# The causal mask of the first score pass moved from TensorE into VectorE's maximum

## The chip, the cores and the metric

The kernel runs on one core of one Trainium2 chip, in one launch. The metric is the device time of that launch in microseconds; the kernel before took 659.16 us (median of three runs, 657.58 to 659.57).

## The reference, cut to what matters

The program is a small network on x of shape 8 x 256 x 16 x 16: a non-local convolution block, a quantised convolution block, and two transformer layers over 256 tokens of 256 channels in each of 8 batches. Both layers attend causally with 16 heads of 16 channels; the first adds a linear bias (ALiBi) before the mask:

```
scores = einsum('bhqd,bhkd->bhqk', q, k) / sqrt(16)   (+ slope_h * (key - query), first layer)
scores = where(key <= query, scores, -inf)
attn   = softmax(scores, axis=-1)
out    = einsum('bhqk,bhkd->bhqd', attn, v)
```

The first layer is followed by a ternary linear layer, the second by a mixture of eight experts with top-2 routing.

## The kernel before, in words

**Two attention passes.** The softmax needs the largest score of each query. The kernel computes the scores twice. The first pass (pieces "S") has queries on the 128 partitions and keys along the free dimension; VectorE reads the scores from PSUM and reduces them to one negated maximum per query and head. These maxima (tile `nmax`) are split into two bf16 parts (pieces "MS", tile `nparts`), turned by TensorE (pieces "M") and copied by ScalarE into extra rows of the stacked queries `QS`. The second pass (pieces "X") has keys on the partitions, includes the negated maximum as one more product row, and ScalarE takes the exponential out of PSUM.

**Units.** The 16 heads form 4 groups of 4. Each group has three units in the first pass, each filling one PSUM bank of 512 columns: part 0 holds the first 128 queries of four heads (128 keys each, as later ones are masked); parts 1 and 2 hold the second 128 queries of two heads each (256 keys each). The mask is a product: TensorE multiplies an identity by a table (`tri0`, `tri1`) of 0 and -1e30 into the bank, and the score products accumulate on top. In parts 1 and 2 this mask product covers the second 128 keys of both heads (256 columns, line 1230); then come two score products of 256 columns (line 1235). One VectorE instruction (line 1467) takes both heads' maxima out of the bank.

**Bodies and the order of work.** There are 16 bodies: 8 batches of layer one ("stage 0", which also carries its ternary layer as stage 1) and 8 of layer two ("stage 2", with the experts as stage 3). The order of each engine's work is written out at build time by `in_order`: every piece has a step, bodies follow each other every 12 steps, and so the pieces of two or three bodies interleave. Each engine runs its own list in order and waits on semaphores. Six PSUM banks are handed round the pieces in TensorE's order: a piece may write its bank only when the one six before has been drained.

**The pieces around the change.** On VectorE, beside S and MS: LNa and LNb (layer norm: statistics at line 1412, 1416 and 1418, a power on GpSimd at line 1136, then the normalised tile `xn` at line 1423); PR and FF (residual additions, line 1494); OX (attention output, lines 1483 and 1484); V (line 1458 or 1460); E (expert sums, line 1547); PAD (constants, once). TensorE transposes `xn` in piece T (line 1176), and the Q, K, V and FF products follow from there (lines 1184 and 1192); expert products are at line 1309, products with V at lines 1266 and 1273.

Of the kernel before, what the change touches and what calls it, by code (L numbers as in the profile page):

```python
# [6 lines left out]
BF16 = mybir.dt.bfloat16  # L7
I32 = mybir.dt.int32
ALU = mybir.AluOpType
ACT = mybir.ActivationFunctionType  # L10
AX = mybir.AxisListType


P = 128
BATCH, CH, IMG = 8, 256, 16
PIX = IMG * IMG
# [19 lines left out]
MASKED = -1e30  # L36
# [174 lines left out]
def build(nc, x_in, fix_in, fixb_in, bias_in, w0_in, w1_in, wt_in, wm_in, parts_dram, out):  # L211
    ctx = ExitStack()
    with ctx:
        def sb(name, shape, dt=F32, c=ctx):
            return c.enter_context(nc.sbuf_tensor(name, shape, dt))
# [16 lines left out]
        def FB(name, lo=0, n=None):  # L232
            at, w = FIXB[name]
            return fixb[:, at + lo:at + lo + (w - lo if n is None else n)]

        def T(name, lo=0, n=None):
            at, w = WT[name]
            return wt[:, at + lo:at + lo + (w - lo if n is None else n)]
# [759 lines left out]
        with ExitStack() as c2:  # L998
            def lb(name, shape, dt=F32):
                return sb(name, shape, dt, c2)  # L1000
# [9 lines left out]
            KS = lb("KS", [P, STACKS, HEADS, PIX], BF16)  # L1010
            V = lb("V", [P, STACKS, 2, HEADS, SLOT])
            nmax = lb("nmax", [P, 2, GROUPS, 2, 4])
            nparts = lb("nparts", [P, 2, 2, P], BF16)
            PT = lb("PT", [P, PT_RING, 512])
            OT = lb("OT", [P, 2, PIX])
# [16 lines left out]
            def wait(eng, name, piece, less=0):  # L1032

                value = COUNTS.after.get((piece, name)) if piece else None
                if value is not None and value - less > asked.get((id(eng), name), 0):
                    asked[id(eng), name] = value - less
                    eng.wait_ge(sems[name], value - less)
# [7 lines left out]
            def full(eng, piece):  # L1045

                wait(eng, f"bank_full{bank_number(piece)}", piece)
# [5 lines left out]
            def bank(piece):  # L1053
                return ps[:, COUNTS.bank[piece], :]

            def drain(piece):
                return sems[f"bank_drained{COUNTS.bank[piece]}"]

            def flat(ap):
                return ap.rearrange("p a n -> p (a n)")  # L1060
# [21 lines left out]
            def stack(stage, batch):  # L1082

                return body(stage, batch) % STACKS
# [10 lines left out]
            def rows_of(stage):  # L1095

                return slice(0, BIAS_AT + (BIAS_ROWS if stage == 0 else 0))
# [65 lines left out]
            def tensor_piece(pe, piece):  # L1163
                kind, stage, batch, n = piece
                par, at = batch % 2, stack(stage, batch)
                if kind in JOBS:

                    drained(pe, piece, 1)
                    d = bank(piece)
# [39 lines left out]
                if kind == "S":  # L1209

                    if n == 0:
                        if piece == ("S", *BODIES[0], 0):
                            pe.wait_ge(fixb_loaded, 16)
                            pe.wait_ge(bias_loaded, 32 * STACKS)
                        first_body = ("PAD", *BODIES[0], 0)
                        wait(pe, "padded", first_body)
                        wait(pe, "chosen", first_body)
                        if stack(stage, batch):
                            wait(pe, "chosen_spread", first_body)
                        for k in range(2):  # L1220
                            wait(pe, f"stack_loaded{k}", ("LOAD", stage, batch, k))
                    g, part = n // 3, n % 3
                    r = rows_of(0) if stage == 0 else slice(0, STACK)
                    if part == 0:
                        pe.matmul(d, FB("ident"), FB("tri0"), start=True, stop=False, skip_group_check=True)
                        for j in range(4):
                            mm = pe.matmul(d[:, j * P:(j + 1) * P], QS[r, at, 4 * g + j, 0:P], KS[r, at, 4 * g + j, 0:P],  # L1227
                                           start=False, stop=(j == 3), skip_group_check=True)
                    else:
                        pe.matmul(d.rearrange("p (j k n) -> p j k n", j=2, k=2)[:, :, 1, :], FB("ident"),  # L1230
                                  FB("tri1").rearrange("p (j n) -> p j n", j=2), start=True, stop=False,
                                  skip_group_check=True)
                        for jj in range(2):
                            h = 4 * g + 2 * (part - 1) + jj
                            mm = pe.matmul(d[:, jj * PIX:(jj + 1) * PIX], QS[r, at, h, P:2 * P], KS[r, at, h, :],  # L1235
                                           start=False, stop=(jj == 1), skip_group_check=True)
                if kind == "M":
                    wait(pe, "max_split", ("MS", *piece[1:]))
                    for t in range(2):
                        mm = pe.matmul(d[:, t * P:(t + 1) * P], nparts[:, n % 2, t], FB("ident"),  # L1240
                                       start=True, stop=True)
                if kind == "X":

                    g, part = n // 3, n % 3
                    r = rows_of(stage)
                    if part == 0:
# [6 lines left out]
                              skip_group_check=True)  # L1253
                    for k, j in enumerate(heads):
                        mm = pe.matmul(d[:, k * width:(k + 1) * width], KS[r, at, 4 * g + j, kt * P:(kt + 1) * P],  # L1255
                                       QS[r, at, 4 * g + j, kt * P:], start=False, stop=(k == len(heads) - 1),
                                       skip_group_check=True)
                if kind == "O0":
# [6 lines left out]
                    for j in range(4):  # L1265
                        pe.matmul(o[32 * j:32 * j + 32, 0:PIX], V[:, at, 0, 4 * n + j, :],  # L1266
                                  PT[:, pt_slot(piece, 3 * n + j // 2), (j % 2) * PIX:(j % 2 + 1) * PIX],
                                  start=True, stop=False, skip_group_check=True)
                if kind == "O1":
                    o = ps[:, 6 + n % 2, :]  # L1270
                    drained(pe, ("X", stage, batch, 3 * n + 2))
                    for j in range(4):
                        mm = pe.matmul(o[32 * j:32 * j + 32, P:PIX], V[:, at, 1, 4 * n + j, :],  # L1273
                                       PT[:, pt_slot(piece, 3 * n + 2), j * P:(j + 1) * P],
                                       start=False, stop=True, skip_group_check=True)
# [23 lines left out]
                if kind == "GB":  # L1299

                    drained(pe, ("GT", stage, batch, 0))
                    for t in range(2):
                        mm = pe.matmul(d[:, t * CH:(t + 1) * CH], gateT[:, t, :], M("be"),
                                       start=True, stop=True)
# [86 lines left out]
            def vector_piece(dve, piece):  # L1391
                kind, stage, batch, n = piece
# [14 lines left out]
                if kind == "LNa":  # L1407
# [3 lines left out]
                    for t in range(2):  # L1411
                        op = dve.bn_stats(stats[:, m, t, :], src[:, t, :])  # L1412
                    settle(op)
                    dve.memset(ve[:, m], EPS)
                    for t in range(2):
                        op = dve.bn_aggr(mv[:, m, t, :], stats[:, m, t, :])
                    settle(op)
                    dve.tensor_tensor(ve[:, m], ve[:, m], mv[:, m, :, 1], ALU.add).then_inc(sems["var_ready"], 1)  # L1418
                if kind == "LNb":
                    wait(dve, "rstd_ready", ("LNa", stage, batch, 0))  # L1420
                    full(dve, ("T", stage, batch - 1, 0))
                    for t in range(2):
                        op = dve.tensor_scalar(xn[:, m, t, :], src[:, t, :], mv[:, m, t, 0:1], rstd[:, m, t:t + 1],  # L1423
                                               ALU.subtract, ALU.mult)
                    op.then_inc(sems["xn_ready"], 1)
                if kind in ("Q", "K"):
                    k = "QK".index(kind)
                    wait(dve, f"first_ready{k}", piece)
                    wait(dve, f"third_ready{k}", previous("SPLIT", stage, batch, k))
                    if stage == 0:  # L1430
                        bias = qk_bias[:, 0 if kind == "Q" else 1]
                        for c in range(NC2):
                            op = dve.scalar_tensor_tensor(rest[:, k, c, :], bank(piece)[:, c * PIX:(c + 1) * PIX],  # L1433
                                                          bias[:, c:c + 1], parts[:, k, 0, c, :], ALU.add, ALU.subtract)
                    else:
                        op = dve.tensor_tensor(flat(rest[:, k]), bank(piece), flat(parts[:, k, 0]), ALU.subtract)  # L1436
# [3 lines left out]
                if kind == "PAD":  # L1440
                    dve.wait_ge(fixb_loaded, 16)
                    rows = slice(MAX_AT, MAX_AT + MAX_ROWS)
                    half = MAX_ROWS // PARTS_OF_MAX
                    dve.tensor_tensor(chosen[rows, :], FB("ident", MAX_AT, half)[rows, :],
                                      FB("ident", MAX_AT + half, half)[rows, :], ALU.add).then_inc(sems["own_rows"], 1)
                    dve.memset(nparts[:], 0.0).then_inc(sems["padded"], 1)
                    dve.memset(gate[:], 0.0).then_inc(sems["padded"], 1)
                    pads = V[:].rearrange("p a t h s -> p (a t h) s")
                    dve.memset(pads[:, :, DH + 1:], 0.0).then_inc(sems["padded"], 1)
                    dve.memset(pads[:, :, DH:DH + 1], 1.0).then_inc(sems["padded"], 1)  # L1450
                if kind == "V":
                    full(dve, piece)
                    full(dve, previous("O1", stage, batch, GROUPS - 1, STACKS))
                    for t in range(2):
                        dst = V[:, stack(stage, batch), t, :, 0:DH]
                        src = bank(piece)[:, t * CH:(t + 1) * CH].rearrange("p (h d) -> p h d", d=DH)
                        if stage == 0:
                            op = dve.tensor_tensor(dst, src, T("bv0").rearrange("p (h d) -> p h d", d=DH), ALU.add)
                        else:
                            op = dve.tensor_copy(dst, src)  # L1460
                    op.then_inc(drain(piece), 1)
                if kind == "S":
                    full(dve, piece)
                    g, part = n // 3, n % 3
                    w_ = P if part == 0 else PIX
                    group = nmax[:, par, g]
                    dve.tensor_reduce(group[:, 0, :] if part == 0 else group[:, 1, 2 * part - 2:2 * part],  # L1467
                                      bank(piece).rearrange("p (j n) -> p j n", n=w_),
                                      AX.X, ALU.max, negate=True).then_inc(drain(piece), 1)
                if kind == "MS":  # L1470
                    wait(dve, "padded", ("PAD", *BODIES[0], 0))
                    for part in range(3):
# [65 lines left out]
                if kind == "E":  # L1538
# [7 lines left out]
                    for k in range(2):  # L1546
                        op = dve.scalar_tensor_tensor(acc[:, t, :], bank(piece)[:, k * CH:(k + 1) * CH],  # L1547
                                                      gate[:, par, t, 2 * e + k:2 * e + k + 1], acc[:, t, :], ALU.mult, ALU.add)
# [5 lines left out]
            with nc.Block() as block:  # L1554
# [16 lines left out]
                @block.tensor  # L1571
                def _(pe):
                    for piece in in_order("tensor"):
                        tensor_piece(pe, piece)
# [6 lines left out]
                @block.vector  # L1581
                def _(dve):
                    for piece in in_order("others"):
                        vector_piece(dve, piece)
# [125 lines left out]
```

## Time and profile before

| | |
|---|---|
| Median of three runs | 659.16 us (657.58 to 659.57) |
| Span of the profiled execution, first to last instruction | 655.6 us |
| Time of that execution outside its span | not recorded; the median lies 3.6 us above the span |
| TensorE matmul busy | 594.0 us, 91% |
| VectorE busy | 445.9 us, 68% |
| ScalarE busy | 327.7 us, 50% |
| GpSimd busy | 117.7 us, 18% |
| Mean granted TensorE clock | 0.973 of full speed |

Engines: PE is TensorE's matmuls, PEld its weight loads, DVE VectorE, ACT ScalarE, POOL GpSimd. "L1230" is line 1230 of the kernel. A busy time counts an instruction from start to end; on TensorE, where products follow each other before the earlier has ended, durations overlap, and the chain of waits shows what one really adds. A "pitch" below is the time from the start of one instruction to the start of the next on the same engine.

### The profile page before, as it was taken

To read this page: it belongs to the slowest core of one execution; us is meant where nothing else is said; L and a number is where in the kernel's file an instruction comes from. 1 tells how busy PE (TensorE), PEld (TensorE's weight loads), DVE (VectorE), ACT (ScalarE), POOL (GpSimd) and SP (SyncE) were. 2 spreads that over 40 slices of the span, in tenths; PEclk is the share of its full clock that TensorE was granted. 3 is DMA by queue.
4 is the path that set the end of the run, shared out by engine and by line. 5 is a ranking of instruction groups with operands and counts; after the bars stand their busy time and mean duration, and the time that the engine had idled before them with its cause. 6 is when DMAs were issued, how large, how long until landed. Compare 5 with 4: busy or idle time off the path is not lost.

```text
span 655.6 us, 11274 instructions
## 1 busy us (share of the span) xinstructions
PE 594.0 (91%) x4177; PEld 407.3 (62%) x4224; DVE 445.9 (68%) x1273; ACT 327.7 (50%) x552; POOL 117.7 (18%) x115
## 2 busy tenths in 40 slices
PE   9875776878999999999999979999999999999897
PEld 4744344656776777777777757576665756565443
DVE  4677768766667668577577575866768476776464
ACT  2356577537566666656566563352443435353110
POOL 2121001341332323312213202020030200000000
PEclk9996998978999999999999989999999999999999
DMA  9500000573315315224224223114050320000000
GB/s 336 222 0 0 1 0 11 144 222 97 108 47 147 98 52 149 85 66 145 78 70 146 61 85 103 44 41 121 0 161 1 91 72 17 1 17 1 16 17 16
DMA packets 40254, 50.66 MB, mean 77 GB/s; under 512 B 4052, under 2 KB 33492, under 8 KB 39892
## 3 DMA queue, kind: packets, MB, share of 16 engines
q1 hardware_dynamic: 40200, 49.94, 25.0%
q8 instruction: 34, 0.56, 0.3%
q14 instruction: 20, 0.16, 0.1%
HBM read 35.11 MB, written 14.68 MB: 76 GB/s over the span
## 4 chain that ended last, share of the span: by engine, by line
PE 60%; DVE 15%; issue 3%; ACT 3%; DMA 1%; SPq 1%; DVEq 0%; POOL 0%; ACTq 0%
PE ps L1309 14%; PE ps L1192 8%; PE ps L1184 7%; PE ps L1266 5%; PE ps L1255 5%; DVE nmax L1467 4%; PE ps L1176 3%; PE ps L1251 3%; PE ps L1235 3%; PE ps L1227 3%; PE ps L1273 2%; DVE acc L1547 2%; PE ps L1230 2%; DVE stats L1412 2%; DVE xn L1423 2%
## 5 line engine op out<-in xcount | busy, mean ns | idle before, releaser
L1467 DVE TENSOR_REDUCE nmax<-ps 128x2 f32<-128x512 f32 (+1 forms) x192 | 130.5, 686 | 78.7 <-PE ps L1235 50.9
L1360 ACT ACTIVATE PT<-ps 128x512 f32<-128x512 f32 x192 | 113.2, 597 | 115.8 <-PE ps L1255 114.1
L1309 PE MATMUL ps<-wm,xnT 128*128 128x512 f32 x256 | 119.9, 599 | 0.7
L1354 ACT ACTIVATE QS<-ps 8x1024 bf16<-8x1024 f32 x64 | 65.0, 1016 | 27.3 <-PE ps L1240 25.3
L1255 PE MATMUL ps<-QS,KS 110*128 110x256 bf16 (+3 forms) x512 | 74.7, 247 | 0.0
L1547 DVE SCALAR_TENSOR_TENSOR acc<-ps,gate,acc 128x256 f32<-128x256 f32 x128 | 61.6, 481 | 18.5 <-PE ps L1309 16.2
L1309 PEld LDWEIGHTS ps<-wm,xnT 128*128 128x128 f32 x256 | 45.1, 190 | 39.7 <-issue 38.1
L1136 POOL TENSOR_TENSOR rstd<-ve,fix 128x2 f32<-128x2 f32 x31 | 21.5, 693 | 258.0 <-DVE ve L1418 258.0
L1184 PE MATMUL ps<-xnT,by_dim 128*128 128x256 f32 x256 | 62.7, 391 | 2.2 <-ACT xnT L1325 2.2
L1156 POOL TENSOR_TENSOR parts<-rest,fix 128x512 bf16<-128x512 f32 x30 | 38.1, 1270 | 138.7 <-DVE rest L1436 99.0
L1251 PE MATMUL ps<-fixb 128*128 128x256 bf16 (+1 forms) x192 | 60.0, 313 | 2.3 <-DVE nmax L1467 2.0
L1184 PEld LDWEIGHTS ps<-xnT,by_dim 128*128 128x128 f32 x256 | 47.5, 194 | 8.5 <-ACT xnT L1325 1.8
L1255 PEld LDWEIGHTS ps<-QS,KS 110*128 110x128 bf16 (+1 forms) x512 | 45.2, 98 | 11.9 <-issue 1.7
L1235 PE MATMUL ps<-KS,QS 110*128 110x256 bf16 (+1 forms) x256 | 49.9, 276 | 0.0
L1192 PE MATMUL ps<-wt,xnT 128*128 128x256 f32 x192 | 45.8, 381 | 0.0
L1266 PE MATMUL ps<-PT,V 128*32 128x256 f32 x512 | 41.3, 395 | 0.0
L1192 PEld LDWEIGHTS ps<-wt,xnT 128*128 128x128 f32 x192 | 34.8, 190 | 4.1
L1230 PE MATMUL ps<-fixb 128*128 128x256 bf16 x128 | 35.7, 279 | 0.9 <-DVE rest L1433 0.9
L1160 POOL TENSOR_TENSOR parts<-rest,parts 128x512 bf16<-128x512 f32 x30 | 34.7, 1155 | 2.4
L1235 PEld LDWEIGHTS ps<-KS,QS 110*128 110x128 bf16 (+1 forms) x256 | 25.6, 100 | 12.4 <-issue 8.3
L1192 PE MATMUL ps<-wt,attnT 128*128 128x256 f32 x128 | 31.5, 389 | 1.1 <-ACT attnT L1325 0.7
L1325 ACT ACTIVATE xnT<-ps 128x512 f32<-128x512 f32 x32 | 19.1, 596 | 26.2 <-PE ps L1176 26.2
(221 smaller groups left out, 918.3 us busy)
## 6 DMA issues: line engine op xcount, KB each, us to landing
parts_dram<-parts SPq DMA_DIRECT2D x32, 384.0 KB, 3.0
QS<-parts_dram SPq DMA_DIRECT2D x96, 128.0 KB
KS<-parts_dram SPq DMA_DIRECT2D x96, 128.0 KB, 2.6
wt<-wt_dram SPq DMA_DIRECT2D x1, 2562.0 KB, 18.7
wm<-wm_dram SPq DMA_DIRECT2D x1, 2449.0 KB, 13.1
xc<-x_dram SPq DMA_DIRECT2D x8, 256.0 KB, 5.5
out_dram<-res SPq DMA_DIRECT2D x8, 256.0 KB, 2.1
w<-w_dram SPq DMA_DIRECT2D x1, 845.0 KB, 7.7
```

What stands on the lines that cost most here:

```text
L1184: mm = pe.matmul(d[:, o * PIX:(o + 1) * PIX], w[:, c, o], src[:, c, :], start=(c == 0), stop=(c == 1))
L1192: mm = pe.matmul(d[:, t * width:(t + 1) * width], src[:, c, t * P:(t + 1) * P], w[:, c * wstep + w_at:c * wstep + w_at + width], start=(c ...
L1230: pe.matmul(d.rearrange("p (j k n) -> p j k n", j=2, k=2)[:, :, 1, :], FB("ident"), FB("tri1").rearrange("p (j n) -> p j n", j=2), start=T ...
L1235: mm = pe.matmul(d[:, jj * PIX:(jj + 1) * PIX], QS[r, at, h, P:2 * P], KS[r, at, h, :], start=False, stop=(jj == 1), skip_group_check=True)
L1251: pe.matmul(d.rearrange("p (j n) -> p j n", n=width)[:, :, 0:P], FB("tri0", 0, P), FB("ident").unsqueeze(1).broadcast_to([P, len(heads), P ...
L1255: mm = pe.matmul(d[:, k * width:(k + 1) * width], KS[r, at, 4 * g + j, kt * P:(kt + 1) * P], QS[r, at, 4 * g + j, kt * P:], start=False, s ...
L1266: pe.matmul(o[32 * j:32 * j + 32, 0:PIX], V[:, at, 0, 4 * n + j, :], PT[:, pt_slot(piece, 3 * n + j // 2), (j % 2) * PIX:(j % 2 + 1) * PIX ...
L1309: mm = pe.matmul(d, normT(stage, batch)[:, c, t * P:(t + 1) * P], M("We", c * EXPERTS * CH + e * 2 * CH, 2 * CH), start=(c == 0), stop=(c ...
L1354: act.activation(QS[MAX_AT:MAX_AT + MAX_ROWS, stack(stage, batch), 4 * n:4 * n + 4, :], bank(piece)[MAX_AT:MAX_AT + MAX_ROWS, 0:PIX].unsqu ...
L1360: act.activation(PT[:, pt_slot(piece, n), :], bank(piece), ACT.Exp).then_inc(drain(piece), 1)
L1467: dve.tensor_reduce(group[:, 0, :] if part == 0 else group[:, 1, 2 * part - 2:2 * part], bank(piece).rearrange("p (j n) -> p j n", n=w_), ...
L1547: op = dve.scalar_tensor_tensor(acc[:, t, :], bank(piece)[:, k * CH:(k + 1) * CH], gate[:, par, t, 2 * e + k:2 * e + k + 1], acc[:, t, :], ...
```

## The change

In parts 1 and 2 of the first score pass (128 units in all) TensorE's mask product is gone, and each score product stands alone. VectorE replaces its one reduction per unit by two instructions, one per head: each adds a mask row `causal` (bf16, 0 for the first 128 keys, the triangle for the second) to the scores of that head, multiplies by -1, writes the result back over the scores in PSUM, and takes the minimum into `nmax`. Part 0 and the second pass keep theirs. The tile `causal` is filled once, in piece PAD, by a memset and a copy.

```diff
+            causal = lb("causal", [P, PIX], BF16)
...
                     else:
-                        pe.matmul(d.rearrange("p (j k n) -> p j k n", j=2, k=2)[:, :, 1, :], FB("ident"),
-                                  FB("tri1").rearrange("p (j n) -> p j n", j=2), start=True, stop=False,
-                                  skip_group_check=True)
                         for jj in range(2):
                             h = 4 * g + 2 * (part - 1) + jj
                             mm = pe.matmul(d[:, jj * PIX:(jj + 1) * PIX], QS[r, at, h, P:2 * P], KS[r, at, h, :],
-                                           start=False, stop=(jj == 1), skip_group_check=True)
+                                           start=True, stop=True)
...
+                    dve.memset(causal[:, 0:P], 0.0)
+                    dve.tensor_copy(causal[:, P:PIX], FB("tri1", 0, P))
...
-                    w_ = P if part == 0 else PIX
                     group = nmax[:, par, g]
-                    dve.tensor_reduce(group[:, 0, :] if part == 0 else group[:, 1, 2 * part - 2:2 * part],
-                                      bank(piece).rearrange("p (j n) -> p j n", n=w_),
-                                      AX.X, ALU.max, negate=True).then_inc(drain(piece), 1)
+                    if part == 0:
+                        op = dve.tensor_reduce(group[:, 0, :], bank(piece).rearrange("p (j n) -> p j n", n=P),
+                                               AX.X, ALU.max, negate=True)
+                    else:
+                        for jj in range(2):
+                            j = 2 * part - 2 + jj
+                            scores = bank(piece)[:, jj * PIX:(jj + 1) * PIX]
+                            op = dve.tensor_tensor_reduce(scores, scores, causal[:],
+                                                          -1.0, -MASKED, ALU.add, ALU.min, group[:, 1, j:j + 1])
+                    op.then_inc(drain(piece), 1)
```

## Rows read from the trace of the kernel before

**Rows 1.** The page: span, busy time of each engine, granted clock in 40 slices.
```profile
span 655.6 us, 11274 instructions
PE 594.0 (91%) x4177; PEld 407.3 (62%) x4224; DVE 445.9 (68%) x1273; ACT 327.7 (50%) x552; POOL 117.7 (18%) x115
...
PEclk9996998978999999999999989999999999999999
```

**Rows 2.** Groups of instructions by line: busy us, mean ns | idle us before.
```profile
L1230 PE MATMUL ps<-fixb 128*128 128x256 bf16 x128 | 35.7, 279 | 0.9 <-DVE rest L1433 0.9
...
L1458 DVE TENSOR_TENSOR V<-ps,wt 128x256 f32<-128x256 f32 x16 | 6.0, 416 | 0.0
```

**Rows 3.** Chain of waits, one stage 0 body: start us, us, what.
```profile
335.44 0.66 DVE xn L1423 x2
...
336.24 0.63 PE ps L1176 x4
336.87 0.11 PE ps L1230
...
337.34 0.28 PE ps L1251
...
350.62 0.39 PE ps L1227 x4
...
358.87 1.21 DVE nmax L1467 x2
...
360.58 0.66 DVE xn L1423 x2
```

**Rows 4.** VectorE in order of time, the same body: start us, us; in brackets idle before.
```profile
336.61 0.68 DVE L1494 TENSOR_TENSOR X<-ps,X 128x512 f32<-128x512 f32 x1
...
351.05 0.69 DVE L1467 TENSOR_REDUCE nmax<-ps 128x4 f32<-128x512 f32 x1 [0.92 <-PE ps L1227]
...
352.38 0.42 DVE L1412 BATCH_NORM_STATS2 stats<-X 128x6 f32<-128x256 f32 x1
352.40 0.06 DVE L1410 MEMSET spare<- 128x1 f32 x1
352.72 0.41 DVE L1412 BATCH_NORM_STATS2 stats<-X 128x6 f32<-128x256 f32 x1
...
353.53 0.68 DVE L1467 TENSOR_REDUCE nmax<-ps 128x2 f32<-128x512 f32 x1
354.41 0.74 DVE L1423 TENSOR_SCALAR xn<-X,mv,rstd 128x256 f32<-128x256 f32 x2 [0.20 <-POOL rstd L1136]
355.06 0.68 DVE L1467 TENSOR_REDUCE nmax<-ps 128x2 f32<-128x512 f32 x1
355.88 0.17 DVE L1476 CAST nparts<-nmax 128x8 bf16<-128x8 f32 x1
```

**Rows 5.** Chain of waits, one stage 2 body.
```profile
426.08 0.65 DVE xn L1423 x2
...
448.48 0.11 PE ps L1230
...
460.80 0.69 DVE nmax L1467
...
465.04 0.65 DVE xn L1423 x2
```

**Rows 6.** Chain of waits before 160 us and after 535 us.
```profile
138.54 1.80 DVE nmax L1467 x3
...
142.18 0.21 PE ps L1230
...
584.58 0.11 PE ps L1230
```

**Rows 7.** VectorE in order of time, before 140 us.
```profile
118.09 0.87 DVE L1433 SCALAR_TENSOR_TENSOR rest<-ps,qk_bias,parts 128x256 f32<-128x256 f32 x2 [1.16 <-ACT parts L1339]
...
137.79 0.75 DVE L1458 TENSOR_TENSOR V<-ps,wt 128x256 f32<-128x256 f32 x2
```

## The prediction

> **What bounds the kernel now.** I read the page first, to see who could be the bound: TensorE is busy 91% of the span at a granted clock near its upper level (2.4 GHz), VectorE 68% [rows 1]. That does not say what the change is worth, for two reasons that the next views show. A busy time on TensorE counts overlapping products: the mask product reads 279 ns in the groups [rows 2], while the chain of waits gives it 0.11 us of its own wherever products follow each other at the upper clock [rows 3, 5]. And the chain changes hands. In a stage 0 body (25.14 us, from one xn at 335.44 to the next at 360.58, both on the chain) TensorE holds it from the transposes at 336.24 to the part 0 scores at 350.62 [rows 3]; then VectorE holds it. The chain prints ScalarE ahead of the maximum's split at 355.88, but in order of time VectorE itself was reducing until 355.74 and had hardly been idle since 351.05: a reduction that waited for TensorE, residual, statistics, a 0.20 us wait for GpSimd's power, xn, another reduction [rows 4]. I take this as the true path. A stage 2 body (38.96 us, xn to xn) has the same two parts, TensorE for about 30 us, then VectorE for about 9 us [rows 5]. So a faster first pass on TensorE helps in one part and a slower reduction hurts in the other.
>
> **Removed.** 128 mask products with their weight loads. Busy time falls by 35.7 us [rows 2], the path by far less. Where VectorE holds the chain, a shorter unit only makes TensorE wait longer: nothing. Counted along the chain in the TensorE parts: before 175 us nine products, three with the clock at its lower level of 1.2 GHz, 3 x 0.21 + 6 x 0.11 = 1.29 us; in each of eight stage 0 bodies four, of which that at 336.87 gives 0.03 only, since the product at 337.34 waits for the residual addition that ends at 337.29 [rows 3, 4]: 8 x (3 x 0.11 + 0.03) = 2.88; as stage 2 sets in, one at the lower clock and five, 0.76; three stage 2 bodies with six each, 1.98; from 537 to 585 us twelve more, where the chain no longer passes a changed reduction, 1.32 [rows 5, 6]. Sum 8.2 us. What covers VectorE's longer instructions in these parts is its own idle time: 0.92 us ahead of the reduction at 351.05 [rows 4].
>
> **Added.** Per unit one 512-column reduction becomes two 256-column instructions, each with a one-column result besides its full output. The reduction's pitch is 0.605 us (1.21 for two) [rows 3]. The nearest row for half of it is the two-source addition out of PSUM for V, 256 columns: 0.75 us for two, of which the last takes 0.416, so a pitch of 0.334 [rows 2, 7]. These two points make a line: 0.27 per 256 columns and 0.063 per instruction. Let d be what a unit costs more.
> The rows of before show no instruction with a result column besides an output. Lower end: the column costs nothing, as a memset between two statistics costs nothing (starts 352.38 and 352.72, a pitch of 0.34) [rows 4]. Then d = 2 x 0.334 - 0.605 = 0.06; I see no reason for less, since two instructions carry the same columns as one. Upper end of the ordinary kind: the column can be written only when the full 0.416 of its instruction is over, plus 0.063: pitch 0.48, d = 0.35. In between: it costs one instruction's fixed 0.063, d = 2 x (0.334 + 0.063) - 0.605 = 0.19. I take 0.19, because the line through the rows charges every operand-reading instruction that much, whatever its size. One more unknown: nothing on VectorE writes into PSUM before, and here output and input are the same bank. If that took two steps a column, another 0.27 per instruction, so d = 0.73 with the middle value.
> The Trainium skill ("VectorE: DVE Perf Modes", section on two Vector instructions with no wait between them) speaks against the change: an op that also writes out its accumulator is two instructions, the main one and an accumulator read. "Vector Engine (DVE) Microarchitecture Reference", section 5.2, puts about 75 ns on each instruction beside the columns. By the two pages an estimate is d = 2 x (0.267 + 0.075 + 0.075) - 0.605 = 0.23 and the sum below +0.3 us in place of -1.2. The trace's 0.063 agrees with the fixed cost; the two instructions no run here shows yet.
>
> **On the path.** Changed reductions that hold the chain: five before 160 us (two of the three at 138.54, three more), two as stage 2 sets in, two in each of three stage 2 bodies (460.80 and one more in the one shown) [rows 5, 6], and in each of eight stage 0 bodies three (355.06 and the two at 358.87) [rows 3, 4]. That is 5 + 2 + 6 + 24 = 37 times d. The one at 353.53 lies beside the wait for GpSimd; at its pitch it is over at 354.13, and xn starts at 354.41, so it costs only what exceeds 0.28. What is queued behind a longer reduction is the split of the maxima and xn, for which TensorE's transposes wait; this is in the count. The other changed reductions fall into idle time.
> Constants: a memset and a copy of 128 columns each, together less than the 0.75 of two 256-column additions, once; VectorE later waits 1.16 us for ScalarE ahead of 118.09 [rows 7]. Nothing, and at most 0.75 us without that cover. No DMA is added or moved, and no queue reordered.
> **Sum:** 37 d - 8.2 + 8 x max(0, d - 0.28). With d = 0.19: 7.0 - 8.2 = -1.2 us on the span of 655.6. The median of the runs is 3.6 us above the span; the profiled execution's own time is not recorded, so I carry the difference over to the median: 659.2 - 1.2 = 658.0. The sum is zero at d = 0.22.
>
> **Rivals.** (a) *The result column is free.* For: the memset between the statistics [rows 4]. Against: that one has no input. d = 0.06 gives 2.2 - 8.2 = -6.0, 653.2 us. (b) *The column waits for the end of its instruction.* Place: VectorE's dense stretch of every stage 0 body, from 351.05 to xn at 360.58 [rows 3, 4]. Price: d = 0.35, 13.0 - 8.2 + 0.6 = +5.4, 664.6 us; it decides from d = 0.28 on, where the sum passes +2.0. For: every small step in that stretch that depends on its predecessor waits for its full duration (the split of 355.88 comes after the 0.68 of 355.06). Against: within one instruction order is kept without a semaphore. (c) *Reading and writing one bank halves the rate:* d = 0.73, 27.0 - 8.2 + 3.6 = +22.4, 681.6 us. Nothing for or against it here. (d) *TensorE's busy share is the bound throughout,* so that VectorE's parts do not matter and all 128 products at 0.11 come off: -14, 645 us. Against it: the stretch of VectorE in every body [rows 4].
>
> **How the numbers follow.** Forecast (d from 0.12 to 0.28): 0.46. (a), d below 0.12: 0.18. (b), d up to 0.5: 0.24. (c): 0.08. (d) and the rest: 0.04. A measurement of this kernel tells 0.3%, 2.0 us, from no change. That is d below 0.17 for faster and above 0.28 for slower. Faster: (a), half of (d), and a third of the forecast's weight: 0.18 + 0.02 + 0.16 = 0.36. Same: 0.30 of the forecast and 0.02 of the rest. Slower: (b) and (c), 0.32. Range: from (a), 653.2, to just past (b), 666: it leaves out (c), the upper part of (b) and (d), some 0.17. The forecast's own range is 655.2 (d = 0.12) to 661.3 (d = 0.28).
>
> **What the changed profile would show.** The mask group of 128 products gone, and with it some 36 us of TensorE's busy time; two instructions per unit on VectorE, four if the column has a row of its own, at a pitch near 0.79 for a unit; the stage 0 body from xn to xn at 25.14 + 3 x 0.19 - 0.36 = 25.35 us, the stage 2 body at 38.96 + 0.38 - 0.66 = 38.68 us: longer in one layer, shorter in the other. A stage 0 body that gets shorter would show (a), one above 25.8 (b) or (c). The prediction is wrong in its path if a unit costs 0.19 and the bodies do not move in opposite directions.

## The result, and the profile after

The changed kernel took 661.09 us (median), against 657.89 us for the kernel before in the same session: 1.0043 times as long, with a 95% interval from 1.0029 to 1.0058, so 1.9 to 3.8 us slower. One of its twenty runs took 1184.13 us; it is left out of the comparison, and no trace shows what happened in it. Measured once more further on, beside other runs of before, the ratio was 1.0061 (1.0040 to 1.0082). The forecast was 1.2 us faster, in a range (653.2 to 666 us) that holds the measured time, with a chance of 0.32 for slower.

The page of the profiled execution (span 660.4, own time 662.21 us; the rows of before are [rows 1]):

```profile
span 660.4 us, 11404 instructions
...
PE 584.7 (89%) x4049; PEld 395.0 (60%) x4096; DVE 468.1 (71%) x1659; ACT 328.4 (50%) x552; POOL 117.8 (18%) x115
```

TensorE has 128 instructions fewer, VectorE 386 more: 256 for the new pairs in place of 128, two constants, and 256 that the code does not name. They stand in the groups, where the mask product [rows 2] is gone and line 1473 has two rows:

```profile
L1473 DVE CUSTOM_DVE_ANT_0 ps<-ps,causal 128x256 f32<-128x256 f32 x256 | 103.2, 448 | 37.5 <-PE ps L1233 37.3
...
L1473 DVE DVE_READ_ACCUMULATOR2_ANT nmax<- 128x1 f32 x256 | 36.2, 142 | 0.0
```

The result column is a row of its own, a read of the accumulator. That much the Trainium skill says ("VectorE: DVE Perf Modes", section on two Vector instructions with no wait between them), and the trace agrees. What the read costs is another question, and 142 ns is not the answer, as VectorE in order of time shows, at the end of one 25 us body (start us, us):

```profile
363.68 0.47 DVE L1473 CUSTOM_DVE_ANT_0 ps<-ps,causal 128x256 f32<-128x256 f32 x1
364.06 0.14 DVE L1473 DVE_READ_ACCUMULATOR2_ANT nmax<- 128x1 f32 x1
364.06 0.47 DVE L1473 CUSTOM_DVE_ANT_0 ps<-ps,causal 128x256 f32<-128x256 f32 x1
364.44 0.14 DVE L1473 DVE_READ_ACCUMULATOR2_ANT nmax<- 128x1 f32 x1
...
365.10 0.17 DVE L1482 CAST nparts<-nmax 128x8 bf16<-128x8 f32 x1
```

Read the starts, not the durations: 363.68, 364.06, and 364.44, where a read and the next main instruction start together. That is 0.38 us from one main instruction to the next, and a pair at 2 x 0.38 = 0.76 us, where the reduction took 0.605. That makes d = 0.16; the prediction took 0.19 (a pitch of 0.79).

The chain of waits of the same body (start us, us, what) answers to [rows 3]:

```profile
339.93 0.73 DVE xn L1421 x2
...
352.18 0.22 PE ps L1233 x2
...
352.84 0.12 issue
352.96 1.97 PE ps L1193 x8
...
365.47 0.65 DVE xn L1421 x2
```

The body takes 365.47 - 339.93 = 25.54 us, others of the same trace 25.46, where before it took 25.14; forecast was 25.35. The body with experts takes 38.80 us in place of 38.96; forecast 38.68. So they moved in opposite directions, as forecast, but each came out worse than forecast by 0.1 to 0.2 us. To place the loss along the whole span, here are rows of the chain in each trace. First the changed kernel, then the kernel before (its first reduction, at 138.54, stands in [rows 6]; the changed kernel's starts at 139.88):

```profile
160.43 0.66 DVE xn L1421 x2
...
365.47 0.65 DVE xn L1421 x2
...
392.88 0.66 DVE xn L1421 x2
...
508.70 0.66 DVE xn L1421 x2
```

```profile
158.09 0.66 DVE xn L1423 x2
...
387.89 0.65 DVE xn L1423 x2
...
504.00 0.66 DVE xn L1423 x2
```

To compare, the terms of the forecast have to be put into the stretches where their rows lie on the chain of before. Of the nine products before 175 us, six (3 x 0.21 + 3 x 0.11 = 0.96, by the lengths of the rows) lie ahead of 158.09 and three in the body behind it. The six that the forecast counted as the second layer sets in (0.76) lie behind 387.89, and one of its three bodies with six each lies behind 504.00.

| stretch | forecast | after - before |
|---|---|---|
| up to the first reduction (138.54) | 0 | +1.3 |
| from there to the first xn on the chain (158.09) | 5 x 0.19 - 0.96 = 0.0 | +1.0 |
| eight 25 us bodies (to 360.58) | 24 x 0.19 - 0.33 - 7 x 0.36 = +1.7 | +2.6 |
| second layer sets in (to 387.89) | 2 x 0.19 - 0.36 = 0.0 | +0.1 |
| three bodies of 38 to 39 us (to 504.00) | 6 x 0.19 - 0.76 - 2 x 0.66 = -0.9 | -0.3 |
| from there to the end | -0.66 - 1.32 = -2.0 | +0.1 |
| sum | -1.2 | +4.8 |

Two of these rows cannot be put down to the change as they stand. The first one moves by as much between two traces of one kernel (138.09 and 139.35 us in the two traces of the kernel that adds the mask twice, below). In the last row the changed kernel is 1.5 us ahead up to the projection of the last phase (508.70 to 618.93, where before takes 504.00 to 615.74), but there TensorE's clock was lower. The chain there, of the changed kernel and of the kernel before:

```profile
618.93 3.42 PE ps L1193 x8
622.35 2.00 PE ps L1307 x4
```

```profile
615.74 1.99 PE ps L1192 x8
617.74 1.73 PE ps L1309 x4
```

The same twelve products took 5.42 us in place of 3.72, so 1.7 us more. The windows that cover them, of the changed kernel and of before, put the granted clock (the third number from the end) at 0.68 of full speed, a mix of the two levels of 2.4 and 1.2 GHz, and at 1.00:

```profile
619.00:624.30 5.30, 5.30 (x13) 3.50 (x14) 0.69 (x1) 0.00 (x0) 0.00 (x0) 0.68 0.00 0
```

```profile
615.70:619.50 3.80, 3.76 (x13) 2.58 (x14) 0.69 (x1) 0.00 (x0) 0.00 (x0) 1.00 0.00 0
```

Without the 1.7 us the last row is 0.1 - 1.7 = -1.6 us. Without both, the change cost 1.0 + 2.6 + 0.1 - 0.3 - 1.6 = +1.8 us where -1.2 was forecast. In the second row the chain of the changed kernel passes eight changed pairs, not the five that were counted: VectorE holds it at 147.26 and from 149.42 on, where TensorE held it before. The granted clock was lower there too (0.79 from 140 to 160 us, where before had 0.83 from 138 to 158), and how much of that row is the clock's was not separated.

### The profile page after: what moved, and what is told of

It reads as the page before. It is cut to its first block, busy times and chain, and to the rows that moved or that the text cites. A ratio compares the mean times of both kernels' runs of the same rounds, so it can differ in the third digit from the quotient of the medians.

```text
span 660.4 us, 11404 instructions
## 1 busy us (share of the span) xinstructions
PE 584.7 (89%) x4049; PEld 395.0 (60%) x4096; DVE 468.1 (71%) x1659; ACT 328.4 (50%) x552; POOL 117.8 (18%) x115
## 4 chain that ended last, share of the span: by engine, by line
PE 52%; DVE 22%; issue 4%; ACT 2%; DMA 1%; SPq 1%; POOL 1%; DVEq 0%; ACTq 0%
PE ps L1307 14%; PE ps L1193 9%; PE ps L1185 7%; DVE ps L1473 5%; PE ps L1264 4%; PE ps L1253 4%; PE ps L1249 3%; PE ps L1233 3%; PE ps L1177 3%; DVE xn L1421 2%; DVE stats L1410 2%; PE ps L1228 2%; DVE nmax L1467 2%; DVE acc L1553 2%; PE ps L1271 2%
## 5 line engine op out<-in xcount | busy, mean ns | idle before, releaser
L1473 DVE CUSTOM_DVE_ANT_0 ps<-ps,causal 128x256 f32<-128x256 f32 x256 | 103.2, 448 | 37.5 <-PE ps L1233 37.3
L1467 DVE TENSOR_REDUCE nmax<-ps 128x4 f32<-128x512 f32 x64 | 43.9, 686 | 24.6 <-PE ps L1228 24.3
L1177 PE MATMUL ps<-fix,xn 128*128 128x128 f32 x128 | 20.3, 281 | 18.9 <-DVE xn L1421 12.5
L1233 PEld LDWEIGHTS ps<-KS,QS 110*128 110x128 bf16 (+1 forms) x256 | 23.1, 100 | 23.0 <-issue 18.2
L1473 DVE DVE_READ_ACCUMULATOR2_ANT nmax<- 128x1 f32 x256 | 36.2, 142 | 0.0
```

What stands on the lines that cost most here:

```text
L1467: op = dve.tensor_reduce(group[:, 0, :], bank(piece).rearrange("p (j n) -> p j n", n=P), AX.X, ALU.max, negate=True)
L1473: op = dve.tensor_tensor_reduce(scores, scores, causal[:], -1.0, -MASKED, ALU.add, ALU.min, group[:, 1, j:j + 1])
```

## The experiments

**The theory** after this comparison: VectorE's longer pair costs about what was forecast where VectorE holds the chain, but TensorE's saving is partly hidden behind other engines. **Rivals:** TensorE's clock falls because it has less to do, and that is the loss; writing the sums back into the PSUM bank that is being read costs time; the read of the accumulator is the cost.

### One side at a time

VectorE's side alone: the changed kernel with the mask product put back, so that the mask is added twice.

```
+    pe.matmul(d.rearrange("p (j k n) -> p j k n", j=2, k=2)[:, :, 1, :], FB("ident"),
+              FB("tri1").rearrange("p (j n) -> p j n", j=2), start=True, stop=False,
+              skip_group_check=True)
     for jj in range(2):
...
-                  start=True, stop=True)
+                  start=False, stop=(jj == 1), skip_group_check=True)
```

> The changed kernel with TensorE's mask product put back ahead of the scores, so that VectorE's new pair runs and TensorE saves nothing; the mask is added twice to the 128 square columns of a head. It prices VectorE's side alone. Theory (the time is lost where VectorE sets the end of the chain, and TensorE's saving is partly shadowed): 37 pitches on the chain x 0.16 us, measured in the changed kernel's trace, is 5.9 us, and about 1 us for the later end of the accumulator's read ahead of what follows: 5 to 8 us slower than before, 3 to 5 us slower than the changed kernel; a stage 0 body from xn to xn 25.14 + 3 x 0.16 + 0.07 = 25.7 us. Rival (the loss is TensorE's lower clock from less work): with TensorE's work as before, within 2 us of before. Rival (writing back into PSUM or the read collides with TensorE only when TensorE runs ahead): between the two, under 4 us.

TensorE's side alone: the kernel before without its mask product (line 1230), VectorE's reduction as it was. This kernel leaves the mask out of those units, and it divides the slopes of the linear bias by 16 so that its sums stay finite; its output is not the reference's, and it serves for its time alone.

> The kernel before with the mask product simply dropped and VectorE's old reduction kept: the first pass then leaves the mask out, and the slopes of the linear bias are divided by 16 so that the sums stay finite. It prices TensorE's side alone. Theory: TensorE's saving is partly shadowed by the X add and by ScalarE's copy of the attention transposes, so 3 to 6 us faster than before, below the 8.2 us of the prediction's sum; a stage 0 body loses 0.2 to 0.25 us of its 25.14, not 0.36. The prediction's own working: 8.2 us faster. Rival (TensorE bounds throughout): 14 us faster. Rival (the granted clock falls with less TensorE work): within 1 us of before, with a clock below that of before.

Measured: the first took 665.96 us, 1.0129 (1.0110 to 1.0149) times before: +8.5 us (7.2 to 9.8). The second took 650.83 us, 0.9897 (0.9879 to 0.9915): -6.8 us (5.6 to 8.0). Both lie a little past the ranges expected (5 to 8, 3 to 6), and the sum, +1.7, is near what the change costs. The rival of the clock falls as the cause of the loss: with less work on TensorE the second kernel's mean granted clock was 0.971 to 0.978, where before had 0.971 to 0.976. The bodies are plainer than the totals, since they are the same in every repetition. Rows of the chain with xn, of the mask on both engines:

```profile
235.11 0.66 DVE xn L1424 x2
...
260.79 0.66 DVE xn L1424 x2
...
429.93 0.66 DVE xn L1424 x2
469.21 0.66 DVE xn L1424 x2
```

and of the kernel without the product (in its 25 us bodies the chain takes the body's other xn, the one at 354.41 in [rows 4]):

```profile
157.86 0.66 DVE xn L1420 x2
...
226.10 0.74 DVE xn L1420 x2
251.02 0.74 DVE xn L1420 x2
...
383.96 0.66 DVE xn L1420 x2
421.86 0.66 DVE xn L1420 x2
460.36 0.66 DVE xn L1420 x2
498.87 0.66 DVE xn L1420 x2
```

VectorE's pairs cost 25.68 - 25.14 = +0.54 us in the one kind of body and 39.28 - 38.96 = +0.32 in the other. Forecast: 3 x 0.19 = 0.57 and 2 x 0.19 = 0.38. TensorE's saving is 25.14 - 24.92 = 0.22 and 38.96 - 38.50 = 0.46. Forecast: 0.36 and 0.66. So in the bodies it is the forecast saving that was too large.

### The change in one half of the units

Which units pay, and which gain? The function `by_vector` says in which units VectorE adds the mask. In one kernel only the units that VectorE held before are changed (48 of 128), in the other only those that TensorE held (80 of 128).

```
+def by_vector(stage, n):
+    return n in ((1, 2, 4, 5) if stage == 0 else (4, 5))
...
+mask = not by_vector(stage, n)
+if mask:
+    pe.matmul(...)
...
-if part == 0:
+if part == 0 or not by_vector(stage, n):
```

(The other kernel has the sets 7, 8, 10, 11 and 1, 2, 7, 8, 10, 11.)

> The change made only in the units that VectorE held in the trace of before: in stage 0 the units 1, 2, 4 and 5 of a body, in stage 2 the units 4 and 5. All other units keep the mask product and the reduction of one instruction. Theory: the pitch costs there, and TensorE's saving there is covered: 4 to 7 us slower than before, 2 to 4 us slower than the changed kernel. Rival (clock, or any cost that goes with the number of converted instructions, 44 of 88 pairs or so): half of the changed kernel's loss, 1 to 2 us slower than before.

> The change made only in the units that TensorE held in the trace of before: in stage 0 the units 7, 8, 10 and 11, in stage 2 the units 1, 2, 7, 8, 10 and 11. Theory: the saving comes there at nearly no cost: 3 to 6 us faster than before, and so faster than both kernels. Rival (a cost that goes with the number of converted instructions): slower than before by 1 to 2 us. Rival (the lower clock): no faster than before, with a granted clock below that of before.

Measured: the first took 665.22 us, 1.0107 (1.0084 to 1.0129), +7.0 us; the second 654.37 us, 0.9945 (0.9926 to 0.9963), -3.6 us. The kernel with fewer changed units loses, the one with more gains, so the cost does not go with their number. The loss is made by 48 units; the same edit in the 80 others is a gain. The counts in the expectation (44 of 88) were wrong; the argument does not rest on them.

### Where the sums are written, and what the read costs

The changed kernel with one operand changed: the sums go to a ring in SBUF.

```
+summed = lb("summed", [P, 8, PIX])
...
-op = dve.tensor_tensor_reduce(scores, scores, causal[:],
+op = dve.tensor_tensor_reduce(summed[:, 4 * (g % 2) + j], scores, causal[:],
```

> The changed kernel with the masked sums written into a ring in SBUF in place of back into their own PSUM bank. Theory (a one-head instruction's length is set by its columns and its read row, not by where it writes): pitch of a pair 0.76 us as in the changed kernel, and its time, 2 to 3.5 us slower than before. Rival (writing back into the bank that is read costs VectorE, or disturbs TensorE's writes into the neighbouring banks): the pitch falls towards 0.67 us and the time by 37 x 0.09 = 3 us, to no difference from before.

And the kernel before with its reduction split in two, the mask product left where it was: the second instruction by itself, with no read.

```
+for jj in range(2):
+    j = 2 * part - 2 + jj
+    op = dve.tensor_reduce(group[:, 1, j:j + 1], bank(piece)[:, jj * PIX:(jj + 1) * PIX],
+                           AX.X, ALU.max, negate=True)
```

> The kernel before with its reduction of two heads split into two reductions of one head each, the mask product left on TensorE: one more instruction per unit, no result column beside an output. It prices the split alone. Theory (two thirds of the pitch come from the result's own read row): the pair's pitch is 0.67 us, d = 0.06, so 37 x 0.06 = 2.2 us slower than before, in a range of 1.5 to 3; the rest of the 8 us that VectorE's side cost is the read row. Rival (the split itself is the cost, the read free): pitch 0.76 us, 6 to 8 us slower than before.

Measured: with the ring 655.58 us, 0.9975 (0.9957 to 0.9992) times before, 4.4 us below the changed kernel by the two ratios (1.6 under before against 2.8 over it). My theory fails here and the rival holds, past its own number: the one operand turned a loss into a small gain. Part of the 4.4 us is the clock, since the ring's trace has the twelve products of the last phase at 3.72 us; the destination's own share shows in the pitch and the bodies below. The split took 660.31 us, 1.0030 (1.0016 to 1.0045): +2.0 us, as expected. What that expectation said of the rest, that it is the read, does not hold. VectorE in order of time, sums to the ring:

```profile
360.48 0.42 DVE L1474 CUSTOM_DVE_ANT_0 summed<-ps,causal 128x256 f32<-128x256 f32 x1
360.83 0.08 DVE L1474 DVE_READ_ACCUMULATOR2_ANT nmax<- 128x1 f32 x1
360.83 0.42 DVE L1474 CUSTOM_DVE_ANT_0 summed<-ps,causal 128x256 f32<-128x256 f32 x1
361.17 0.08 DVE L1474 DVE_READ_ACCUMULATOR2_ANT nmax<- 128x1 f32 x1
...
361.73 0.17 DVE L1483 CAST nparts<-nmax 128x8 bf16<-128x8 f32 x1
```

and the split reduction, four in one merged row:

```profile
360.95 1.41 DVE L1473 TENSOR_REDUCE nmax<-ps 128x1 f32<-128x256 f32 x4
362.49 0.17 DVE L1482 CAST nparts<-nmax 128x8 bf16<-128x8 f32 x1
```

Four starts of the split lie in 1.41 us, of which the last takes 0.417 (its group's mean): a pitch of (1.41 - 0.417) / 3 = 0.33 us. With the mask operand and the read, sums to SBUF, it is (361.17 - 360.48) / 2 = 0.345. With the sums back into PSUM it is 0.38. Per pair, against the reduction's 0.605: the second instruction 0.06, operand and read together 0.02 to 0.03, the PSUM destination 0.07; in sum the 0.16 of the changed kernel. Whether any PSUM bank as destination would cost this, or only the one that is being read, no run here tells. The read itself also shrinks from 0.14 to 0.08 us, and the split of the maxima, which waits for it, follows the start of the last main instruction by 0.56 us (361.17 to 361.73) in place of 0.66 (364.44 to 365.10). The bodies follow: 25.18 us with the ring (261.25 to 286.43), which is 25.14 + 3 x 0.085 - 0.22.

The Trainium skill ("Perfetto Trace Analysis", section on optimizing Scalar and DVE operations) gives an instruction of VectorE about 125 ns of access overhead on PSUM against 60 on SBUF. It does not say whether the source or the destination counts. The direction agrees for the destination, at 35 ns of pitch here, in a kernel that reads PSUM in both cases.

### Choosing the units body by body

```
+def by_vector(stage, batch, n):
+    at = body(stage, batch)
+    held_by_vector = (1, 2, 4, 5) if at < 10 else (4, 5) if at < 14 else ()
+    return n not in held_by_vector + (11,)
```

> The selection of the run with TensorE's units, mended body by body: bodies 8 and 9, which are the first two of the second layer, ran at the 25 us pitch and had their units 1 and 2 changed although VectorE holds them there; here these two stay as before. In the last two bodies, where the chain passes hardly a reduction, units 4 and 5 are changed as well. Unit 11, whose mask product stands in the hole that TensorE waits for ScalarE's copy of the attention transposes, stays as before in all bodies. Theory: the 25 us bodies take 24.92 us, all of them, with unit 11's product at no cost; the 39 us bodies stay at 38.50; in all 3.5 to 5 us faster than before. Rival (every mask product on TensorE is worth its 0.11 us, so leaving 16 of them back costs 1.8 us): 25 us bodies at 25.03, 39 us bodies at 38.61, in all 2 to 3 us faster than before.

Measured: 652.72 us, 0.9918 (0.9896 to 0.9940): 5.4 us (3.9 to 6.8) faster than before, a little past the 3.5 to 5 expected. No kernel here that keeps the mask is faster beyond the noise. The bodies came out as expected, 24.92 and 38.50 us, although unit 11 kept its product; if every product were worth its 0.11 us, they would have been 25.03 and 38.61. Its chain over one such body shows why; at the point where the changed kernel had 0.12 us of "issue" the product (line 1239 here) stands again:

```profile
334.35 0.65 DVE xn L1432 x2
...
346.51 0.11 PE ps L1239
...
347.29 0.01 issue
347.29 1.97 PE ps L1199 x8
...
359.26 0.65 DVE xn L1432 x2
```

The projection (line 1199 here, 1193 in the changed kernel, 1192 before) needs ScalarE's copy of the turned attention output (tile `attnT`). That copy in the changed kernel, then the copy and the chain in the kernel before:

```profile
352.21 0.60 ACT L1323 ACTIVATE attnT<-ps 128x512 f32<-128x512 f32 x1 [0.57 <-PE ps L1177]
```

```profile
347.86 0.60 ACT L1325 ACTIVATE attnT<-ps 128x512 f32<-128x512 f32 x1 [0.68 <-PE ps L1176]
```

```profile
347.82 0.11 PE ps L1230
...
348.60 1.97 PE ps L1192 x8
```

In the changed kernel the copy ends at 352.21 + 0.60 = 352.81 and the projection starts at 352.96. In the kernel before the copy ended at 347.86 + 0.60 = 348.46 and the projection started at 348.60, with the mask product in between. The copy sets the time in both, 0.14 us after its end. Take the product out and the hole shows.

Then both findings together, this selection with the ring:

> The selection by body with the masked sums written into the SBUF ring: both findings together. Theory (in the units that are changed here VectorE waits for TensorE anyway, so a shorter pair is worth nothing; only the first two bodies and the last two could gain some tenths): within 2 us of the selection by body alone, so 4 to 7 us faster than before; 25 us bodies at 24.92 us, 39 us bodies at 38.50. Rival (writing into PSUM also disturbs TensorE, whose banks it shares): the bodies get shorter by another 0.1 to 0.3 us and the whole by 2 us or more.

Measured: 653.24 us, 0.9922 (0.9895 to 0.9950), the same as the selection alone, with bodies of 24.92 and 38.50 us again. So a shorter pair is worth nothing in the units that are left, as the theory had it: VectorE waits there anyway. The rival, a disturbance of TensorE by the writes into PSUM, would have shortened the bodies.

### The spells at the lower clock

> The kernel that adds the mask on both engines, once more for a second trace: its other runs were some 4 us longer than the one that was profiled. Theory (spells at the lower clock level come and go, in the last phase above all): a run that is longer has its extra time in a stretch at 1.2 GHz that the first trace did not have, with the bodies between 160 and 500 us at 25.67 and 39.28 us as there. Rival (the first profiled run was odd in its bodies): longer bodies at a full clock.

Measured: 665.08 us, span 663.3 where the first trace had 660.0. The bodies agree within 0.01 us (25.67 and 39.27 in the second), so the theory of spells holds, but not their place: from 504 us to the end the two agree to 0.1 us. The 3.3 us are 1.3 before the first reduction, 0.7 from there to the first xn, and 1.4 in the body after it, where windows of both traces show the clock. First trace, then second (us, busy time of TensorE, its weight loads, VectorE, ScalarE, GpSimd; granted clock, DMA share, GB/s):

```profile
161.00:169.00 8.00, 7.95 (x76) 6.56 (x66) 4.08 (x15) 4.91 (x11) 2.42 (x2) 1.00 0.01 2
```

```profile
161.00:169.00 8.00, 8.00 (x73) 5.97 (x74) 2.81 (x12) 4.64 (x9) 1.27 (x1) 0.81 0.00 0
```

> The changed kernel once more, beside the same runs of before and for a second trace. Theory: the 25 us bodies at 25.46 to 25.54 us and the 39 us bodies at 38.80 as in the first trace, since they do not depend on the spells at the lower clock level; what differs from the first trace lies before 165 us and after 590 us, where those spells are. In all 2 to 4 us slower than before. Rival (the loss is the clock): bodies that move with the clock of the run.

Measured: 662.58 us, 1.0061 (1.0040 to 1.0082), bodies of 25.45 and 38.80 us, and again a clock of 0.68 beside the projection of the last phase (window from 619.3 to 624.7 us). Over both sets, and without the run of 1184 us, 11 of the changed kernel's 27 runs have a mean granted clock of 0.966 and take 662.2 to 663.4 us; the other 16, at 0.968 to 0.974, take 658.6 to 661.4. Both traces come from runs of the first kind, so that the late spell is what sets them apart is likely, but not shown. The other 16 average 660.2 us, still 2.3 above the mean of the runs of before (657.9). The spell is worth 1.7 us in the traces that have it, and it is not tied to the loss: the traces of the mask on both engines, slower than the changed kernel, run at 1.00 there, while the faster kernel with TensorE's units has a stretch of 0.58 from 612 us on.

## Why the prediction was wrong

**What bounds the kernel: right.** The chain changes hands within each body; a body without experts got longer, one with experts shorter, and the two half changes went apart by 7.0 + 3.6 = 10.6 us.

**Added, d: right in size, by a wrong reason.** d = 0.19 was forecast and 0.16 measured. The 37 pitches came out well: 0.54 us per 25 us body for 0.57, 0.32 for 0.38, and over all stretches behind the first reduction 6.4 and 7.1 us in the two traces of the mask on both engines (the early spell of the second left out), for 7.0. That the sizes met so closely is in part luck: I charged the read of the result column 0.063 us, and it costs at most 0.015 with the sums in SBUF. Rival (a), the column that is free, was nearly true. What made up the rest was the destination in PSUM, the one that the prediction set aside for rival (c) at 0.27 us per instruction and which is 0.035. By the Trainium skill ("VectorE: DVE Perf Modes", section on two Vector instructions with no wait between them, and "Vector Engine (DVE) Microarchitecture Reference", section 5.2) the estimate was d = 0.23; the measured 0.16 decides.

**Removed: the step that failed.** "Counted along the chain in the TensorE parts" gave 8.2 us. The kernel without the product saves less in every stretch (the forecast's terms are placed as in the first table):

| stretch | forecast saving | in the trace |
|---|---|---|
| first reduction to first xn | 0.96 | 0.6 (19.55 to 18.96) |
| eight 25 us bodies | 2.85 | 1.8 (8 x 0.22) |
| second layer sets in | 0.36 | 0.2 |
| three bodies of 38 to 39 us | 2.08 | 1.2 |
| after 504 us | 1.98 | 1.6 |
| sum | 8.2 | 5.4 |

The second row takes 0.22 for all eight bodies, though the trace has seven of them at that and the first one 1.95 us shorter than before's (26.50 to 24.55 between the reductions that end it). There the clock differs: windows of before, then of the kernel without the product, have it at 0.62 and at 1.00. The changed kernel's trace is low there as before's is (0.79 from 161 to 169 us, where before has 0.87), so that body's other 1.7 us is left out of the table.

```profile
160.00:164.00 4.00, 4.00 (x45) 2.19 (x42) 0.78 (x2) 2.46 (x5) 0.09 (x1) 0.62 0.00 0
```

```profile
160.00:164.00 4.00, 3.95 (x49) 2.92 (x43) 1.21 (x4) 2.73 (x6) 0.00 (x0) 1.00 0.00 0
```

A spell that one run has and another has not moves a total by as much, so the 6.8 us between the medians is no clean measure of the saving either.

A product on the chain was counted as its full 0.11 us. I checked this for one place only, the residual addition at 337.29, and not for the projection 11 us later, which waits for ScalarE's copy. There the product filled a hole, and its 0.11 us came back as idle time; at the residual addition the 0.03 did not come either. Of four products in a 25 us body two count, 0.22 for 0.36. A body with experts has the same hole, 0.11 us idle ahead of its projection, which leaves 0.55 of 0.66; 0.46 was measured, most of the rest at one attention product that lasts 0.19 on the chain for 0.11 before, and why it does was not traced. Nor were the first and the last stretch taken apart product by product. With 5.4 in place of 8.2 the forecast's own VectorE term gives 7.0 - 5.4 = +1.6, near the +1.8 that the trace shows outside the first 138 us and the late spell. The sign was lost there.

**What the text did not have:** spells at the lower clock, which differ between runs of one kernel by more than the whole effect forecast. They are the likely reason for the gap between +1.8 us in the trace without its spell and +2.8 or +4.0 in the two medians: the second set has five of its eight runs at the clock of 0.966, the first six of nineteen. None of the 13 runs of before beside the second set is under 0.968. Why the changed kernel has such runs is open.

**Rivals.** (b) is out: at d = 0.35 a 25 us body would have passed 25.8. (c) has the right place, the destination, and an eighth of its size (0.035 for 0.27); that reading and writing the same bank is the reason was not shown. (d) is out by the half changes, and by the 6.8 us of the kernel without the product, where 14 were forecast.

## What to carry to other kernels

A product, copy or add that stands on the chain is worth its time only if nothing else ends with it. Before counting a saving, look at each step behind it for a second thing that it waits for: the saving counts only down to the end of that one. And an edit that shifts work from one engine to another is chosen unit by unit: ask of each which engine holds the chain there, and make it only where the engine that gives the work away holds it; here this was the difference between 0.4% slower and 0.8% faster.

## What the runs showed of the hardware that was not expected

- With the sums written to SBUF, reading the accumulator added at most 0.015 us to the pitch of a 256-column instruction (0.345 against 0.33 for a reduction without it), although its row lasts 0.08 us: it lies beside the next instruction.
- The same instruction with its output in PSUM had a pitch of 0.38 us, and the read behind it, which writes to SBUF in both kernels, lasted 0.14 us in place of 0.08.
- TensorE's clock fell to 0.68 of full speed beside the last phase's projection in both traces of the changed kernel, and not in that of before, after stretches that look alike: TensorE was busy 3.04 us of the 5.5 us ahead of it in the changed kernel, and 2.99 of 5.4 us before, at a granted clock of 1.00 in both. What decides was not found.
